# Head outputs turned by VectorE straight from a rotating output bank, in an attention and mixture-of-experts layer on one Trainium2 core

## The chip, the cores and the metric

One core of a Trainium2 chip runs the whole program. The metric is device time in microseconds (us) for one execution; a lower time is better. A timed run carries no profile. The profile is one further execution of the same program, taken by the hardware profiler, and its span is read on that execution alone.

Names used throughout: PE is TensorE (PEld its weight loads), DVE is VectorE, ACT is ScalarE, POOL is GpSimd, SP is SyncE, which here only issues DMAs. PSUM has eight banks of 128 partitions by 512 fp32 numbers.

## What is computed

Two sequences of 2048 tokens with 256 features pass through layer norm, 16-head attention (head dimension 16) with a local mixing term, and then a routed mixture of four experts. Cut to what matters here:

```python
Q, K, V = heads(x @ Wq.T + bq), heads(x @ Wk.T + bk), heads(x @ Wv.T + bv)
A = softmax(Q @ K.T / sqrt(16))                    # 2 sequences x 16 heads, 2048 x 2048 each
out = (0.6 * A + 0.4 * L) @ V                      # L: a fixed band of 7 tokens around the diagonal
x = x + out @ Wo.T + bo
x = x + experts(layernorm(x))                      # router, top 2 of 4 experts
```

The 32 pairs of a sequence and a head are called heads below.

## The kernel before

`project` (L153) normalises the tokens, projects Q and K and writes them in two pieces (a high and a low part in a short fp32 form) to a DRAM buffer `qk_pieces` (L232). `attend` (L367) then runs the 32 heads, two per pass of a loop, and `route_and_experts` does the rest.

For one head, `attend` goes through 16 steps `kb`, one for each 128 keys. In a step PE makes four score tiles (L763: 128 keys by 512 queries, chunks c = 0 to 3), which ACT exponentiates from PSUM into `probs` (L681), and multiplies the step's `probs` with the values (L775), adding into one output bank over the 16 steps. Four groups of 512 queries use four groups of 32 output partitions: 16 features, and 16 rows of ones that give the softmax sum. Score tiles rotate through three PSUM banks, so a tile waits for the exponential of the tile three before it. Scores are made one step ahead of the values.

The softmax needs the largest score of each query first. PE makes those scores as well (L750, two pairs per step, in four further banks, two for each pair) and DVE takes the row maxima of each pair with one reduction (L626). They run 21 steps ahead (`LOOK`): at step `kb` of head n, PE and DVE work on group kb + 5 of head n + 1. So at step 10 all 16 groups of head n + 1 are done; DVE combines and negates them (`split_shift`, L634), and POOL splits the result into two pieces (`split_shift`, L586 and L588). This `shift` (128 queries by 32 columns) must become rows of the score operand `score_q`, so it is transposed at the end of step 12 (`SHIFT_AT`): by PE (L782) into a score bank, copied by ACT to `shift_row` (L686), and written by four DMAs into `score_q` (`load_shift`, L484, `SHIFT_DMAS`). PE waits for these DMAs (`shift_in`, L842) at the start of step 15, where the scores of the next head begin.

At a head's end ACT copies the output bank to `heads_sb` (`copy_o`, L696), and PE's first values of the next head wait for that copy (L772). After step 1 (`HEADS_AT`) PE transposes `heads_sb` in four blocks of 128 x 128 (L786) into a score bank, and ACT copies it to `heads_tok` (`copy_tok`, L692). After the maxima of step 2 DVE inverts the softmax sums (`invert`, L642), and POOL multiplies them in (`normalise`, L597).

Every engine runs its own program in order, and the order is written out by hand; semaphores tie the programs together. SP issues, in order and per head: 12 loads of maximum operands, a store and two loads of weight chunks, the four shift DMAs, and 12 loads of score operands.

Of the kernel before, what the change touches and what calls it, by code (L numbers as in the profile page):

```python
# [152 lines left out]
def project(nc, ctx, dram, keep, block):  # L153
# [46 lines left out]
    def _(sp):  # L200
# [21 lines left out]
        for seq in range(BATCH):  # L222

            with sp.Fori(seq * BPS // 2, (seq + 1) * BPS // 2) as i:
                for u in range(2):
                    n = 2 * i + u
                    for qk in range(2):
                        for m in range(KD):
                            sp.wait_ge(piece_lo, QK * n + 2 * qk + m + 1)
                            head = seq * HEADS + m * (HEADS // KD)  # L230
                            dst = dram["qk_pieces"][qk, head:head + HEADS // KD, :, :, ds((n % BPS) * BLOCK, BLOCK)]
                            sp.dma_start(dst.rearrange("h d c t -> (h d) c t"),  # L232
                                         pieces[u][:, qk, m, :, :].bitcast(F32)).then_inc(stored[u], 16)
# [98 lines left out]
    def _(pe):  # L332
# [14 lines left out]
        def body(i, first, last):  # L347
            for u in range(2):
                n = 2 * i + u
                pe.wait_ge(xnT_ready, n + 1)  # L350
                for qk in range(2):
                    if qk == 1 and not (last and u):
                        transposes(n + 1, 1 - u)
                    for m in range(KD):
# [3 lines left out]
                        for k in range(KD):  # L358
                            done = nc.tensor.matmul(ps_qk[j], w["qk"[qk]][:, k, m * P:(m + 1) * P],
                                                    xnT[:, ds(n, 1), k, :].squeeze(1),  # L360
# [6 lines left out]
def attend(nc, ctx, dram, keep, block):  # L367
# [25 lines left out]
    heads_sb = sb("heads_sb", [P, BLOCK])  # L393
    heads_tok = sb("heads_tok", [P, BLOCK])
    part_max, neg_max, shift, shift_row = (keep[n] for n in ("part_max", "neg_max", "shift", "shift_row"))
    inv_sum = sb("inv_sum", [P, ST])
    w_raw = sb("w_raw", [P, CHUNK])
    w_pair = sb("w_pair", [P, 2, CHUNK], F32R)
    psum = keep["psum"]
    ps_s = [psum[:, c, :] for c in range(3)]  # L400
    ps_o = psum[:, 3, :]
    ps_m = [psum[:, 4:6, :], psum[:, 6:8, :]]

    ps_tr = psum[:, 7, :]
    ps_shift = ps_s[2][0:PIECES * ST, 0:P]
# [3 lines left out]
    UNITS = CH * ST + 2  # L409
    HEADS_AT = 1  # L410

    def unit(n, kb, c, ends=False):

        after = (kb > HEADS_AT + 1) + (kb > SHIFT_AT + 1 and not ends)
        return n * UNITS, CH * kb + c + after

    def heads_unit(n):
        return n * UNITS, CH * (HEADS_AT + 2)

    def shift_unit(n):  # L420
        return n * UNITS, CH * (SHIFT_AT + 2) + 1

    def count_of(at):
        return at[0] + at[1] + 1

    def bank_of(at):
        return ps_s[at[1] % RING]
    SHIFT_DMAS = PIECES * ROW_TILES
# [17 lines left out]
    first_tr, first_copied = sem("first_shift_tr"), sem("first_shift_copied")  # L446
    s_ready, exp_done = sem("s_ready"), sem("exp_done")
    pv_done = sem("pv_done")
    o_copied = sem("o_copied")
    inv_ready = sem("inv_ready")  # L450
    last_tr, last_copied = sem("last_tr"), sem("last_copied")
# [9 lines left out]
    SHIFT_HALF = 2 * (ST + 1)  # L461
# [9 lines left out]
    BANKS_BEFORE_SHIFT = v_tiles_before(SHIFT_HALF) // 2  # L471
    ps_v = [ps_s[r % VB] for r in range(BANKS - 1)] + [ps_o]
# [6 lines left out]
    def _(sp):  # L479
        def load_shift(u):  # L480
            for h in range(ROW_TILES):
                for c in range(PIECES):
                    row, first = h * ROW_TILE + STACK + c, c * ST + h * ST // ROW_TILES
                    sp.dma_start(score_q[u][row:row + 1, :].bitcast(F32).rearrange("o (t q) -> o t q", q=P),  # L484
                                 shift_row[first:first + ST // ROW_TILES, :].bitcast(F32)).then_inc(shift_in[u], 16)
# [11 lines left out]
        sp.wait_ge(first_copied, 1)  # L497
# [17 lines left out]
        def body(i, last):  # L515
            for u in range(2):
# [8 lines left out]
                if not (last and u):  # L525
                    sp.wait_ge(exp_done, count_of(shift_unit(n)))
                    load_shift(1 - u)
                if not last:
                    sp.wait_ge(s_ready, count_of(unit(n, ST - 1, CH - 1)))
# [5 lines left out]
    def _(pool):  # L535
# [11 lines left out]
        nc.gpsimd.memset(heads_sb[:], 1.0).then_inc(o_copied, 1)  # L547
        pool.wait_ge(o_copied, 1)
# [31 lines left out]
        def split_shift(m):  # L580
            pool.wait_ge(shift_step, m + 1)
            if m == 1:
                pool.wait_ge(first_tr, 1)
            elif m > 1:
                pool.wait_ge(s_ready, count_of(shift_unit(m - 2)))
            nc.gpsimd.tensor_copy(shift[:, 0, :], neg_max[:]).then_inc(shift_hi, 1)  # L586
            pool.wait_ge(shift_hi, m + 1)
            nc.gpsimd.tensor_tensor(shift[:, 1, :], neg_max[:], shift[:, 0, :].bitcast(F32), ALU.subtract  # L588
                                    ).then_inc(shift_ready, 1)

        def normalise(n):
            tok = heads_tok[:].rearrange("p (c b e) -> p c b e", c=BT, b=BPS)
            inv = inv_sum[:].rearrange("p (c b) -> p c b", c=BT)
            pool.wait_ge(inv_ready, n + 1)
            out = o_sb[:, (n - 1) // HEADS, :, (n - 1) % HEADS, :] if n > 0 else keep["spare"]
            out = out.rearrange("p (b c) d -> p c b d", c=BT)
            nc.gpsimd.tensor_tensor(out, tok[:, :, :, 0:HD], inv.unsqueeze(3).broadcast_to([P, BT, BPS, HD]),  # L597
# [23 lines left out]
    def _(dve):  # L621
# [15 lines left out]

        def invert(n):
            tok = heads_tok[:].rearrange("p (c b e) -> p c b e", c=BT, b=BPS)
            inv = inv_sum[:].rearrange("p (c b) -> p c b", c=BT)  # L640
            dve.wait_ge(exp_done, count_of(heads_unit(n)))
            nc.vector.reciprocal(inv, tok[:, :, :, HD]).then_inc(inv_ready, 1)  # L642

        for t in range(ST):
# [3 lines left out]
        nc.vector.tensor_copy(shift[:, 0, :], neg_max[:]).then_inc(shift_hi, 1)  # L648
        dve.wait_ge(shift_hi, 1)
        nc.vector.tensor_tensor(shift[:, 1, :], neg_max[:], shift[:, 0, :].bitcast(F32), ALU.subtract  # L650
                                ).then_inc(shift_ready, 1)
        for t in range(LOOK - ST):
            maxima(ST + t, t)

        def body(i, last):
            for u in range(2):
                n = 2 * i + u
                for kb in range(ST):
# [3 lines left out]
                    if kb == HEADS_AT + 1:  # L662
                        invert(n)
# [1089 lines left out]
```

## Time and profile before

| | before |
|---|---|
| timed runs, median of 3 | 1990.95 us (1990.76 to 1991.04) |
| span of the profiled execution | 2006.8 us |
| PE busy | 1951.3 us, 97% of the span |
| DVE busy | 1626.5 us, 81% |
| ACT busy | 1374.2 us, 68% |
| POOL busy | 346.9 us, 17% |

The profiled execution took 2006.8 us from its first to its last instruction, 15.9 us (0.8%) more than the median of the timed runs. The busy shares are means over stages with different limits: the attention heads run from about 130 us to 1431 us, the projections before and the experts after. Matmuls are pipelined and their ends are modelled, so the starts of instructions tell more than their durations.

### The profile page before, as it was taken

Reading aid. Unit: us, or ns where it says so; the run is one execution under the profiler, and the core shown is the slowest. Engines: PE = TensorE matmul, PEld = TensorE weight load, DVE = VectorE, ACT = ScalarE, POOL = GpSimd, SP = SyncE. Lnnn points to the kernel's source line nnn. Section 1 sums busy time; section 2 is a strip of 40 time slices with the busy share of each in tenths; the row PEclk is TensorE's granted clock in tenths of the full one; section 3 lists DMA queues with packets and bytes.
Section 4 is the critical chain, followed back from the end, with each engine's and each line's share of the span. In section 5 each row is a group of like instructions: output and inputs, shape, how many; then the busy total and the mean of one; then the engine's idle time right before and its main releaser. Section 6 shows DMA issues by size and latency. Waiting matters only on the chain. (4 is left out here: it accounts for less than half of the span.)

```text
span 2006.8 us, 47862 instructions
## 1 busy us (share of the span) xinstructions
PE 1951.3 (97%) x16384; PEld 1036.7 (52%) x16384; DVE 1626.5 (81%) x2075; ACT 1374.2 (68%) x2471; POOL 346.9 (17%) x379
## 2 busy tenths in 40 slices
PE   7999999999999999999999999999998799999997
PEld 3543333333333333333333333333687689999997
DVE  6799999999999999999999999994255565555564
ACT  3358888888888888888888888889544422233332
POOL 1361010001000100001000100010024532232233
PEclk9999999999999999999999999999999899999999
DMA  7954355335643454336534554341123677788884
GB/s 266 245 111 92 78 102 115 74 74 97 108 90 74 90 99 106 74 80 102 113 74 74 100 105 90 74 93 54 42 74 131 242 235 227 245 269 297 263 272 113
DMA packets 105849, 264.09 MB, mean 132 GB/s; under 512 B 20896, under 2 KB 52768, under 8 KB 99104
## 3 DMA queue, kind: packets, MB, share of 16 engines
q1 hardware_dynamic: 92624, 245.29, 48.6%
q0 software_dynamic: 13152, 17.83, 4.6%
q8 instruction: 44, 0.72, 0.1%
q14 instruction: 29, 0.24, 0.0%
HBM read 206.95 MB, written 73.94 MB: 140 GB/s over the span
## 5 line engine op out<-in xcount | busy, mean ns | idle before, releaser
L626 DVE TENSOR_REDUCE part_max<-psum 128x1 f32<-128x1024 f32 x1024 | 1240.8, 1222 | 50.6 <-PE psum L750 37.7
L681 ACT ACTIVATE probs<-psum 128x512 f32<-128x512 f32 x2048 | 1111.1, 596 | 145.4 <-PE psum L763 78.2
L763 PE MATMUL psum<-score_q,score_k 50*128 50x512 f32 x2048 | 745.9, 446 | 0.1
L750 PE MATMUL psum<-max_k,max_q 48*128 48x512 f32 x2048 | 737.9, 449 | 0.5 <-DVE part_max L626 0.4
L775 PE MATMUL psum<-probs,v_ones 128*32 128x256 f32 x8192 | 654.1, 391 | 9.4 <-ACT heads_sb L696 9.0
L763 PEld LDWEIGHTS psum<-score_q,score_k 50*128 50x128 f32 x2048 | 306.9, 184 | 404.7 <-ACT probs L681 390.7
L775 PEld LDWEIGHTS psum<-probs,v_ones 128*32 128x32 f32 x8192 | 162.1, 107 | 380.8 <-issue 198.1
L750 PEld LDWEIGHTS psum<-max_k,max_q 48*128 48x128 f32 x2048 | 294.2, 185 | 12.8 <-issue 7.0
L1184 ACT ACTIVATE x_sb<-psum,x_sb 128x512 f32<-128x512 f32 (+1 forms) x160 | 101.6, 636 | 257.8 <-PE psum L1564 243.1
L1583 PE MATMUL psum<-w,h_hi 128*128 128x256 f32 x1120 | 202.1, 279 | 2.7 <-DVE h_lo L1385 2.5
L1583 PEld LDWEIGHTS psum<-w,h_hi 128*128 128x128 f32 x1120 | 178.7, 189 | 13.8 <-DVE h_lo L1385 3.2
L1383 DVE CAST h_hi<-x_sb 128x512 fp32r<-128x512 f32 (+1 forms) x160 | 66.2, 414 | 129.2 <-ACT x_sb L1184 127.3
L1583 PE MATMUL psum<-w,h_lo 128*128 128x256 f32 x560 | 156.0, 278 | 0.0
L586 POOL CAST shift<-neg_max 128x16 fp32r<-128x16 f32 x31 | 6.1, 198 | 580.7 <-DVE neg_max L634 580.7
L1583 PEld LDWEIGHTS psum<-w,h_lo 128*128 128x128 f32 x560 | 105.3, 188 | 0.0
L1385 DVE TENSOR_TENSOR h_lo<-x_sb,h_hi 128x512 fp32r<-128x512 f32 (+1 forms) x160 | 100.2, 626 | 5.5
L1564 PE MATMUL psum<-w_end,w 128*128 128x512 f32 (+1 forms) x320 | 95.2, 379 | 2.2 <-ACT x_sb L1184 2.2
L1564 PE MATMUL psum<-route_xT_hi,w 128*128 128x512 f32 (+1 forms) x320 | 90.3, 363 | 0.0
L1121 POOL DMA_INDIRECT out<-x_sb,token x36 | 56.7, 1575 | 136.8 <-DVE x_sb L1403 95.5
L1121 POOL DMA_INDIRECT out<-attnT,token x34 | 53.5, 1574 | 140.1 <-DVE attnT L1403 93.4
L551 POOL COPY v_ones<-v_sb 128x256 f32<-128x256 f32 x32 | 12.8, 398 | 336.0 <-PE psum L775 335.8
L1097 POOL DMA_INDIRECT xs<-xrow,slot_at x64 | 63.4, 990 | 32.1 <-issue 19.7
(185 smaller groups left out, 1352.3 us busy)
## 6 DMA issues: line engine op xcount, KB each, us to landing
w<-w_split SPq DMA_DIRECT2D x40, 2048.0 KB, 7.9
max_q<-qk_pieces SPq DMA_DIRECT2D x192, 128.0 KB, 7.2
score_k<-qk_pieces SPq DMA_DIRECT2D x192, 128.0 KB, 4.7
xs<-in_pads SPq DMA_DIRECT2D x33, 528.0 KB, 8.3
qk_pieces<-pieces SPq DMA_DIRECT2D x32, 512.0 KB, 4.6
w_split<-w_pair SPq DMA_DIRECT2D x32, 512.0 KB, 8.8
max_k<-qk_pieces SPq DMA_DIRECT2D x192, 64.0 KB, 8.2
score_q<-qk_pieces SPq DMA_DIRECT2D x192, 64.0 KB, 2.2
```

Source lines behind the costliest of these rows:

```text
L626: nc.vector.tensor_reduce(part_max[:, t, p:p + 1], ps_m[p].rearrange("q b f -> q (b f)"), axis=AXIS.X, op=ALU.max).then_inc(m_read, 1)
L681: nc.scalar.activation(probs[kb % 2][:, chunk * BLOCK:(chunk + 1) * BLOCK], bank_of(at), ACT.Exp, scale=float(HD) ** -0.5).then_inc(exp_do ...
L750: last = nc.tensor.matmul(ps_m[p][:, h, :], max_q[u][rows, t * P:(t + 1) * P], max_k[u][rows, p * BLOCK:(p + 1) * BLOCK], start=True, stop ...
L763: nc.tensor.matmul(bank_of(at), score_k[u][rows, kb * P:(kb + 1) * P], score_q[u][rows, part * BLOCK:(part + 1) * BLOCK], start=True, stop ...
L775: last = nc.tensor.matmul(ps_o[QUAD * j:QUAD * (j + 1), at:at + BLOCK // PARTS], v_ones[u][:, kb, :], probs[kb % 2][:, j * BLOCK + at:j * ...
L1097: nc.gpsimd.indirect_dma_start(dram["xs"], bass.IndirectOffsetOnAxis(ap=at, axis=0), xrow[i % XROWS][:, t, :], None).then_inc(scattered[i ...
L1121: nc.gpsimd.indirect_dma_start(dram["out"], bass.IndirectOffsetOnAxis(ap=token[i % TOKEN_SETS][:, t:t + 1], axis=0), y[u][:, t, :], None, ...
L1184: nc.scalar.activation(h[m % H][:, 0:n], ps_h[m % PS_H][:, 0:n], ACT.Gelu, bias=biases[i % 2][:, m:m + 1]).then_inc(gelu_done, 1)
L1383: nc.vector.tensor_copy(h_hi[m % HALVES][:, 0:n], h[m % H][:, 0:n]).then_inc(h_hi_ready, 1)
L1385: nc.vector.tensor_tensor(h_lo[m % HALVES][:, 0:n], h[m % H][:, 0:n], h_hi[m % HALVES][:, 0:n].bitcast(F32), ALU.subtract).then_inc(h_lo_r ...
L1564: last = nc.tensor.matmul(ps_h[m % PS_H][:, 0:n], w[u][:, 2 * k + m // 4, c, at:at + P], xx[:, k, 0:n], start=j == 0, stop=j == len(terms) ...
L1583: last = nc.tensor.matmul(ps_y[u][:, t // 2, (t % 2) * DIM:(t % 2 + 1) * DIM], hs[m % HALVES][:, toks], w[u][:, chunk, c, at:at + DIM], st ...
```

## The change

VectorE's transpose turns each block of 32 x 32 by itself. The change makes that usable and drops the transposes by TensorE and the copies by ScalarE around them:

- The queries of a head are stored in another order: the Q projection reads its 512 tokens in an order that puts the 32-token quarters of the four 128-token tiles side by side, and each Q store goes to four separate stretches of 128 tokens instead of one of 512. Queries that are 32 apart in a block of the output bank are then the ones that VectorE's blocks need.
- The output bank alternates between PSUM banks 2 and 3 with the head (`OUT_OF`), and the three score banks rotate around it (`FIRST_RING`, `RING_OF`). `copy_o`, the four transposes of `heads_sb`, `copy_tok` and `heads_sb` go. VectorE turns the output bank into `heads_tok` (`turn_heads`) after the maxima of step 15, and inverts the sums after the maxima of the next head's step 0.
- PE's third score tile of step 1 (issued in step 0) takes the bank that held the last head's output and waits for `heads_turned`. The second tile of step 1 waits for the exponential of the tile two before it, where the others wait for the one three before.
- The shift is turned by VectorE too (`turn_shift`, after the maxima of step 12), with no copy by ScalarE. The result lies on 128 partitions, so `load_shift` has eight DMAs of 16 pieces of 128 bytes where it had four of eight pieces of 512 bytes.

```diff
-                            dst = dram["qk_pieces"][qk, head:head + HEADS // KD, :, :, ds((n % BPS) * BLOCK, BLOCK)]
...
+                            if qk == 0:
+                                dst = rows.rearrange("p c (j n) -> p c j n", j=BPS)[:, :, :, ds((n % BPS) * P, P)]
+                                src = src.rearrange("p c (j n) -> p c j n", j=BPS)
...
+                            if qk == 0:
+                                rows = rows.rearrange("p (b j r) -> p j b r", b=BT, j=BPS)
...
+    FIRST_RING, RING_OF, OUT_OF = ((0, 1, 2), (1, 0, 3)), ((1, 0, 3), (0, 1, 2)), (2, 3)
...
+    SHIFT_DMAS = ROW_TILES * P // QUAD
...
         def load_shift(u):
+            n = PIECES * ST // ROW_TILES
             for h in range(ROW_TILES):
-                for c in range(PIECES):
-                    row, first = h * ROW_TILE + STACK + c, c * ST + h * ST // ROW_TILES
-                    sp.dma_start(score_q[u][row:row + 1, :].bitcast(F32).rearrange("o (t q) -> o t q", q=P),
-                                 shift_row[first:first + ST // ROW_TILES, :].bitcast(F32)).then_inc(shift_in[u], 16)
+                row = h * ROW_TILE + STACK
+                dst = score_q[u][row:row + PIECES, :].bitcast(F32).rearrange("c (t q) -> c t q", q=P)
+                for q in range(P // QUAD):
+                    sp.dma_start(dst[:, :, q * QUAD:(q + 1) * QUAD],
+                                 shift_row[q * QUAD + h * n:q * QUAD + (h + 1) * n, :]).then_inc(shift_in[u], 16)
...
-                    sp.wait_ge(exp_done, count_of(shift_unit(n)))
+                    sp.wait_ge(shift_turned, n + 2)
                     load_shift(1 - u)
...
+        def turn_shift(m):
+            dve.wait_ge(shift_ready, m + 1)
+            nc.vector.transpose(shift_row[:], shift[:].rearrange("p h c t -> p (h c t)").bitcast(F32)
+                                ).then_inc(shift_turned, 1)
+
+        def turn_heads(n, u):
+            dve.wait_ge(pv_done, ST * (n + 1) + PV_OPEN)
+            dve.wait_ge(tok_used, n + 1)
+            nc.vector.transpose(heads_tok[:].rearrange("p t e -> p (t e)"), out_bank(u)).then_inc(heads_turned, 1)
...
-                    if kb == HEADS_AT + 1:
+                    if kb == INVERT_AT:
                         invert(n)
                     if ahead == ST - 1 and not (last and u):
                         split_shift(n + 1)
+                    if kb == SHIFT_AT and not (last and u):
+                        dve.wait_ge(shift_in[u], 16 * SHIFT_DMAS * (i + 1))
+                        turn_shift(n + 1)
+                turn_heads(n, u)
...
-        def copy_shift(at):
-            act.wait_ge(s_ready, count_of(at))
-            nc.scalar.activation(shift_row[:], bank_of(at)[0:PIECES * ST, 0:P], ACT.Copy).then_inc(exp_done, 1)
...
-        def copy_o(n):
-            act.wait_ge(pv_done, ST * (n + 1) + PV_OPEN)
-            nc.scalar.activation(heads_sb[:], ps_o, ACT.Copy).then_inc(o_copied, 1)
...
+        def scores(n, kb, u, c):
+            if kb == 1 and c == RING - 1:
+
+                pe.wait_ge(heads_turned, n + 1)
+            else:
+
+                held = 2 if kb == 1 and c == 1 else RING
+                if not isinstance(n, int) or s_done(n, kb, c) > held:
+                    pe.wait_ge(exp_done, s_done(n, kb, c) - held)
...
-                    if kb == HEADS_AT:
-                        wait_bank(heads_unit(n))
-                        pe.wait_ge(o_copied, n + 1)
-                        transpose_heads(bank_of(heads_unit(n))).then_inc(s_ready, 1)
-                    if kb == SHIFT_AT and not ends:
-                        wait_bank(shift_unit(n))
-                        wait_apart(pe, count, shift_ready, n + 2, ones_set, POOL_SET)
-                        transpose_shift(bank_of(shift_unit(n))[0:PIECES * ST, 0:P]).then_inc(s_ready, 1)
```

## Rows read from the trace of the kernel before

**Rows 1.** Windows: us, then busy us of each engine, clock, DMA share, GB/s.
```profile
600.00:800.00 200.00, 198.60 (x1917) 74.74 (x1909) 192.08 (x168) 176.05 (x330) 16.45 (x30) 1.00 0.48 93
60.00:80.00 20.00, 20.00 (x62) 10.11 (x60) 9.54 (x14) 8.17 (x12) 0.00 (x0) 1.00 1.05 396
```
**Rows 2.** The page's groups: busy us, mean ns of one, idle before, releaser.
```profile
L626 DVE TENSOR_REDUCE part_max<-psum 128x1 f32<-128x1024 f32 x1024 | 1240.8, 1222 | 50.6 <-PE psum L750 37.7
L750 PE MATMUL psum<-max_k,max_q 48*128 48x512 f32 x2048 | 737.9, 449 | 0.5 <-DVE part_max L626 0.4
```
**Rows 3.** PE timeline at a head's end: start, us, engine, line, idle before.
```profile
699.32 0.50 PE L763 MATMUL psum<-score_q,score_k 50*128 50x512 f32 x1
...
699.66 0.40 PE L763 MATMUL psum<-score_q,score_k 50*128 50x512 f32 x1
700.33 0.64 PE L775 MATMUL psum<-probs,v_ones 128*32 128x256 f32 x8 [0.27 <-ACT heads_sb L696]
700.90 0.50 PE L763 MATMUL psum<-score_q,score_k 50*128 50x512 f32 x1
```
**Rows 4.** PE timeline around the two transposes by TensorE.
```profile
691.68 0.28 PE L782 MATMUL psum<-ident_sb,shift 128*32 128x128 f32 x1
691.89 0.50 PE L763 MATMUL psum<-score_q,score_k 50*128 50x512 f32 x1
...
704.62 0.66 PE L786 MATMUL psum<-ident_sb,heads_sb 128*128 128x128 f32 x4
705.20 0.50 PE L763 MATMUL psum<-score_q,score_k 50*128 50x512 f32 x1
```
**Rows 5.** Timeline of DVE: maxima, the inversion, the combined maximum.
```profile
690.12 2.35 DVE L626 TENSOR_REDUCE part_max<-psum 128x1 f32<-128x1024 f32 x2
698.85 2.46 DVE L626 TENSOR_REDUCE part_max<-psum 128x1 f32<-128x1024 f32 x2
708.35 0.24 DVE L642 RECIPROCAL inv_sum<-heads_tok 128x16 f32<-128x16 f32 x1
728.64 4.62 DVE L626 TENSOR_REDUCE part_max<-psum 128x1 f32<-128x1024 f32 x4
```
**Rows 6.** Lines by form: a DVE instruction that reads 512 columns of PSUM.
```profile
L1363 DVE TENSOR_TENSOR route_xT_lo<-psum,route_xT_hi 128x512 fp32r<-128x512 f32 x3 | 2.1, 691 | 1.2 <-ACT route_xT_hi L1158 1.2
```
**Rows 7.** Timeline of the shift's way: ACT's copy, SP's four issues, PE's step 15.
```profile
692.00 0.27 ACT L686 ACTIVATE shift_row<-psum 32x128 fp32r<-32x128 f32 x1
692.29 2.73 SPq L484 DMA_DIRECT2D score_q<-shift_row  x4
696.84 0.50 PE L763 MATMUL psum<-score_q,score_k 50*128 50x512 f32 x1
```
**Rows 8.** Lines of SP's DMA issues: ns min/median/max, first and last start.
```profile
L484 SPq DMA_DIRECT2D score_q<-shift_row x128: 620/634/842, 119.6 to 1385.9; - x128
L122 SPq DMA_DIRECT2D max_k<-qk_pieces x192: 315/316/423, 54.2 to 1318.0; - x192
DMA to landing us min/median/max: 2.0/5.9/9.3
```
**Rows 9.** Windows around the last packets of the four shift DMAs.
```profile
695.60:695.90 0.30, 0.30 (x6) 0.29 (x4) 0.30 (x1) 0.30 (x1) 0.00 (x0) 1.00 0.06 14
```
**Rows 10.** ACT timeline: the last exponentials of a head, and the copy behind them.
```profile
698.61 1.09 ACT L681 ACTIVATE probs<-psum 128x512 f32<-128x512 f32 x2 [0.15 <-PE psum L763]
699.58 0.60 ACT L696 ACTIVATE heads_sb<-psum 128x512 f32<-128x512 f32 x1
```
**Rows 11.** PE timeline and windows behind the attention: two long idle stretches, the clock.
```profile
1575.32 1.22 PE L1513 MATMUL psum<-route_xT_hi,w_r_hi 128*128 128x512 f32 x2 [2.64 <-ACT rh L1165]
1609.78 0.50 PE L1583 MATMUL psum<-w,h_hi 128*128 128x256 f32 x2 [2.54 <-DVE h_lo L1385]
1574.88:1578.29 3.41, 2.97 (x7) 2.39 (x8) 2.24 (x13) 0.97 (x2) 2.68 (x3) 0.50 0.81 281
1609.00:1612.40 3.40, 2.62 (x17) 2.45 (x18) 3.30 (x8) 0.69 (x1) 2.48 (x4) 1.00 0.92 305
```

More of the change, by code:

```diff
@@ L408, in attend, with s_done, score_bank, out_bank @@
     RING = 3
[L409 to L428, printed above, removed]
+    UNITS = CH * ST
+    INVERT_AT = 0
+    FIRST_RING, RING_OF, OUT_OF = ((0, 1, 2), (1, 0, 3)), ((1, 0, 3), (0, 1, 2)), (2, 3)
+    def s_done(n, kb, c):
+        return n * UNITS + CH * kb + c + 1
+    def score_bank(u, kb, c):
+        at = CH * kb + c
+        return psum[:, FIRST_RING[u][at % RING] if at < CH else RING_OF[u][(at - CH) % RING], :]
+    def out_bank(u):
+        return psum[:, OUT_OF[u], :]
+    SHIFT_DMAS = ROW_TILES * P // QUAD
     PARTS = 2
@@ L469, in v_tiles_before @@
         return spread if half < FIRST_SCORES else min(TILES, TILES - 2 + half - FIRST_SCORES)
-    BANKS_BEFORE_SHIFT = v_tiles_before(SHIFT_HALF) // 2
-    ps_v = [ps_s[r % VB] for r in range(BANKS - 1)] + [ps_o]
+    ps_v = [psum[:, r % VB, :] for r in range(BANKS - 1)] + [psum[:, OUT_OF[1], :]]
     def v_tiles(b, vb):
@@ L701, in copy_v @@
                                  ).then_inc(v_copied, 1)
-        with act.Fori(0, BANKS_BEFORE_SHIFT // VB) as b:
+        with act.Fori(0, BANKS // VB - 1) as b:
             for vb in range(VB):
-                copy_v(b, vb, ps_s[vb])
-        for r in range(BANKS_BEFORE_SHIFT // VB * VB, BANKS - 1):
-            if r == BANKS_BEFORE_SHIFT:
-                act.wait_ge(first_tr, 1)
-                nc.scalar.activation(shift_row[:], ps_shift, ACT.Copy).then_inc(first_copied, 1)
-            copy_v(r // VB, r % VB, ps_v[r])
+                copy_v(b, vb, ps_v[vb])
+        copy_v(BANKS // VB - 1, 0, ps_v[0])
         for c in range(CH):
-            exp(0, 0, c, False)
+            exp(0, 0, 0, c)
             if c == 1:
-                copy_v((BANKS - 1) // VB, (BANKS - 1) % VB, ps_o)
+                copy_v(BANKS // VB - 1, 1, ps_v[BANKS - 1])
         def body(i, last):
@@ L779, in values @@
                 last.then_inc(pv_done, 1)
-        def transpose_shift(out):
-            return nc.tensor.transpose(out, shift[:].rearrange("p c t -> p (c t)").bitcast(F32), ident[:])
-        def transpose_heads(out):
-            for c in range(BT):
-                last = nc.tensor.transpose(out[:, c * P:(c + 1) * P], heads_sb[:, c * P:(c + 1) * P], ident[:])
-            return last
         def project_v(r, t):
@@ L829, in body @@
                 n = 2 * i + u
-                ends = last and u == 1
                 pe.wait_ge(v_in, n + 1)
@@ L843, in body @@
                     if more_scores:
-                        scores(*nxt, 0, ends)
+                        scores(*nxt, 0)
                     if more_maxima:
@@ L847, in body @@
                     if more_scores:
-                        scores(*nxt, 1, ends)
-                    values(n, kb, u, 0, ends)
+                        scores(*nxt, 1)
+                    values(n, kb, u, 0)
                     if more_scores:
-                        scores(*nxt, 2, ends)
+                        scores(*nxt, 2)
                     if more_maxima:
@@ L854, in body @@
                     if more_scores:
-                        scores(*nxt, 3, ends)
-                    values(n, kb, u, 1, ends)
-                    if kb == HEADS_AT:
-                        wait_bank(heads_unit(n))
-                        pe.wait_ge(o_copied, n + 1)
-                        transpose_heads(bank_of(heads_unit(n))).then_inc(s_ready, 1)
-                    if kb == SHIFT_AT and not ends:
-                        wait_bank(shift_unit(n))
-                        wait_apart(pe, count, shift_ready, n + 2, ones_set, POOL_SET)
-                        transpose_shift(bank_of(shift_unit(n))[0:PIECES * ST, 0:P]).then_inc(s_ready, 1)
+                        scores(*nxt, 3)
+                    values(n, kb, u, 1)
         twice(pe, pairs, body)
```

114 lines of the change are left out of this document (39 added, 75 removed).

## Prediction

> **What bounds the kernel now.** I read the windows first, to see which engine has room in the stage that the change touches. In the attention, PE is busy 198.6 of 200 us and DVE 192.1 [rows 1], which looks like two engines at their limit. The page's groups and DVE's timeline take that apart. PE waited for DVE's maxima 0.4 us in all, and DVE for PE 37.7 us [rows 2]. Two of DVE's reductions in the steady stretch take 2.46 us together; with 1.22 us for one [rows 2] they start 1.24 us apart. Four behind the combined maximum, which made DVE late, take 4.62 us and so start (4.62 - 1.22) / 3 = 1.13 us apart [rows 5]: DVE can catch up by 0.1 us at each. So PE sets the pace, at about 1.24 us for half a step (two score tiles, one maximum pair, half the values), and 32 halves are 39.7 us. The shift DMAs of 32 heads start from 119.6 to 1385.9 us [rows 8], 40.8 us per head. The difference of 1.1 us is what PE does or waits for besides. That is the stake of the change: per head it can win this, and not the busy time of ACT, which lies beside PE.
>
> **What goes, part by part.** At a head's end the half step from 699.32 to 700.90 us takes 1.58 us, with an idle of 0.27 us until ACT's copy is done [rows 3]: 0.34 us over a plain half. The four transposes of the heads take from 704.62 to 705.20: 0.58 us. The transpose of the shift takes 0.21 us, from 691.68 to 691.89 [rows 4]. Together 1.13 us per head on the path that sets the end. ACT's copies give nothing beyond that except in the last head, where no maxima run and ACT sets the pace: two copies, about 0.5 us of issue distance each, so 1 us once. At the very end one more group of four transposes goes, 0.5 us.
>
> **What the head's end costs after it.** The second score tile of step 1 now needs the exponential of the tile two before it, the last one of step 0. ACT's last pair of exponentials ends at 698.61 + 1.09 = 699.70 [rows 10]; today that tile's matmul starts at 699.66. From the end of ACT's copy, 700.18 [rows 10], to the values that waited for it, 700.33 [rows 3], pass 0.15 us; so the tile can start at 699.85, and 0.2 us are lost. A gain is excluded, since the tile waits for more than now; above, 0.34 us bounds it, today's wait, which had ACT's copy in front as well.
>
> The turn of the output bank is one DVE instruction over 128 x 512 of PSUM, which the trace does not show. The nearest row takes 0.69 us for 512 columns out of PSUM [rows 6]; twice the price per column would be 1.23. DVE reaches it when the last reduction of step 15 ends, the first of the two from 698.85, at 700.08 [rows 5], by which time the head's last values are long through; so the wait for them costs nothing. Turned at 700.77, it frees the bank that PE's third tile wants at 700.90 - 0.34 + 0.20 = 700.76: just hidden. Queued behind it on DVE are the maxima of the next step, 0.7 us late; their banks are wanted one half step later, and DVE's 0.1 us per half step pays it back. At twice the price PE would wait 0.55 us per head. The inversion (0.24 us) only moves from step 2 to step 0, and `normalise` on POOL with it, which has a whole head of time.
>
> **What the shift costs.** This is the part that decides. Today ACT's copy ends at 692.27, SP issues four DMAs from 692.29 for 2.73 us, and PE starts step 15 at 696.84 without a wait [rows 7]. One issue takes 0.634 us (0.620 to 0.842) [rows 8], so they lie (2.73 - 0.63) / 3 = 0.70 us apart, and the last begins at 694.39. Its packets still move after 695.6 [rows 9], 1.2 to 1.5 us later; other loads on this queue landed after 2.0 us at the least [rows 8]. I take 1.8 us, keep 1.4 to 2.2, and so have the four landed at 696.2, 0.6 us before they are wanted.
>
> After the change DVE reaches the turn when the maxima of step 12 are read, at 690.12 + 2.35 = 692.47 [rows 5]. A short DVE instruction, the inversion, takes 0.24 us from 708.35 [rows 5]; part of it can lie beside the reduction before, so the turn adds 0 to 0.24, I take 0.16. SP starts 0.02 us later, as behind ACT today: 692.65. It now issues eight DMAs, not four. At 0.70 us each the last begins at 692.65 + 7 x 0.70 = 697.55 and lands at 699.35. PE, 0.21 us earlier than today, stands at step 15 at 696.63. PE waits 2.7 us, and with it everything: the score tiles of the next head are the first thing in step 15, and the maxima, the values, DVE and ACT are all queued behind them. Nothing covers this.
>
> The price of one issue is the unknown: the new ones have other shapes (16 pieces of 128 bytes, two destination rows). The cheapest issues of this queue take 0.315 us [rows 8]; with the same 0.07 us between them the last lands at 697.1 and PE waits 0.5 us. At 0.842 it is 700.8, and 4.2 us. I take 0.634, the row of the same two tensors. The Trainium skill speaks against the change here: "DMA: Bandwidth & Descriptors", section "Rules for kernel authors", asks to coalesce many small transfers, since below 64 KB mostly overhead is paid. The change splits the same 16 KB into twice as many.
>
> The wait occurs at 30 heads. For the last head DVE has no maxima after step 10, so its turn comes two steps earlier. SP's later loads slide by some 3 us and have tens of microseconds.
>
> **Small things.** The first shift has eight DMAs too, with DVE turning about 1 us earlier than ACT copied: I add 1 us. The Q stores move 512-byte pieces where they moved 2 KB; the DMA share is 1.05 from 60 to 80 us, while PE stays busy throughout [rows 1]: 0 to 3 us, I take 0.5.
>
> **The sum.** 30 x 2.7 = 81.0; 31 x (0.20 - 1.13) = -28.8; the 32nd group of head transposes -0.6, ACT in the last head -1.0, the end -0.5, the first shift 1.0, the Q stores 0.5. That is +51.6 us on the profiled execution, whose span of 2006.8 us stands 0.8% over the median; I add it to the median unscaled: 2043.
>
> **The clock.** PE has no idle stretch like 2.7 us in the attention today. Behind it there are some. After 2.64 us of idle the granted clock was 0.50, the level of 1.2 GHz, from 1574.88 to 1578.29; after 2.54 us it stayed at 1.00 [rows 11]. One such stretch of 3.4 us at half the clock costs PE, which is the bound here, 1.7 us of work. With one row each way I can only bound it: 0 to 30 times 1.7, 0 to 51 us. I take a third of the heads, as PE is otherwise never idle here, so +17: 2060.
>
> **The rivals.**
> - Faster: the eight issues are cheap. Place: SP between steps 12 and 15. Without any wait the sum is 51.6 - 81.0 = -29.4, so it decides at a wait of 29.4 / 30 = 1.0 us, which is a distance of 0.45 us per issue. At the cheapest row's 0.38 the wait is 0.5 us: 30 x 0.5 - 29.4 = -14, so 1977. For it: 315 ns rows on the same queue. Against: 128 issues of this very transfer never took less than 620. Chance 0.11.
> - Faster still: the issues don't count at all and the wait stays hidden, 2043 - 81 = 1962. The Trainium skill has this rule, "DMA: Bandwidth & Descriptors", section "Issuing engines are not separate DMA queues": the sequencer's time to start a DMA is usually small beside the DMA. The rows of this transfer speak against it, 0.63 us of issue for 4 KB. Chance 0.03.
> - The head's end becomes the bound: the turn costs twice as much and PE waits 0.55 us more per head, 31 x 0.55 = 17, 2077 with the wait for the shift. It lies inside the forecast's range.
> - The clock falls at every wait: 2043 + 51 = 2094. With the dearest issues (30 x 1.5 more) beyond 2106. Chance of over 2106: 0.06.
> - The change does its work but the terms cancel, a wait of about 1.0 us: 1991, chance 0.03.
>
> **How the numbers follow.** The forecast, eight issues at the row's price and the clock falling at none to all heads, has the remaining 0.77. The range: from 2043 down by 12 for the early landing (30 x 0.4) and by 25 for issues some 0.12 us cheaper, 2006; up by 51 for the clock and by 12 for the late landing, 2106. A measurement of this kernel can tell about 0.2% from no change, 4 us. Faster 0.14, same 0.03, slower 0.83.
>
> **What would show it.** Right: PE idle 2 to 3 us once per head at L763's first tile of step 15, released by the shift DMAs; heads 42 to 44 us apart; 1.24 us per half step elsewhere; no idle over 0.4 us at the head's end; DVE no dearer than 0.7 us for the turn; stretches at half clock behind some of the waits. Wrong: SP's eight issues within 3 us, or heads 40 us apart; then the price of an issue was the failed step. A wait of PE for `heads_turned` would show the turn's price wrong.

## The result and the profile after

| | before | after |
|---|---|---|
| median of the runs, us | 1990.86 | 2241.32 (four runs, 2200.30 to 2267.90) |
| span of the profiled execution, us | 2006.8 | 2266.1 (that run: 2267.90) |

The change makes the kernel slower: the ratio is 1.113, 95% interval 1.105 to 1.121. The four runs of after differ by 3%, and their mean granted clock with them (0.871 in the profiled run of 2267.90 us, 0.906 in that of 2200.30); the ratio and its interval are of the two shortest, 2200.30 and 2232.51 us. The forecast was 2060 us, 2006 to 2106. Its sign was right and its size wrong: about 180 us more were lost by the median. The profile of after, like those of the experiments and unlike that of before, belongs to one of the timed runs.

The page of the kernel after: the span, the busy lines, PE and its granted clock in 40 slices, then two groups (busy us, mean ns of one, idle before, releaser).

```profile
span 2266.1 us, 47389 instructions
...
PE 2159.4 (95%) x16220; PEld 1080.6 (48%) x16220; DVE 1648.4 (73%) x2139; ACT 1340.0 (59%) x2374; POOL 346.4 (15%) x379
...
PE   8999999999999999999999999999999989999997
...
PEclk9998767687988877779879996878899999999999
...
L740 PE MATMUL psum<-score_q,score_k 50*128 50x512 f32 x2048 | 874.2, 511 | 72.6 <-DMA score_q<-shift_row 72.5
...
L725 PE MATMUL psum<-max_k,max_q 48*128 48x512 f32 x2048 | 852.5, 512 | 0.8 <-DVE part_max L620 0.8
```

Three things are to be seen. The wait that was forecast is there: 72.5 us in front of the score tiles, released by the shift DMAs, 72.3 of them in 30 waits of 2.34 to 2.55 us. PE is busy nearly all the same, 95% of a span that is 13% longer. And one maxima matmul, which took 449 ns before [rows 2], now takes 512 in the mean. The clock line, in tenths of full speed, says why: it falls below 9 in most slices of the attention.

One head shows how this hangs together. First the way of the shift on DVE and SP's queue, then PE (start, us, engine, line, idle before in brackets):

```profile
1225.29 0.20 DVE L634 STREAM_TRANSPOSE shift_row<-shift 128x32 f32<-128x32 f32 x1
...
1225.52 5.27 SPq L484 DMA_DIRECT2D score_q<-shift_row  x8
```

```profile
1227.08 0.50 PE L740 MATMUL psum<-score_q,score_k 50*128 50x512 f32 x1
...
1228.32 0.50 PE L740 MATMUL psum<-score_q,score_k 50*128 50x512 f32 x1
...
1231.97 0.49 PE L740 MATMUL psum<-score_q,score_k 50*128 50x512 f32 x1 [2.34 <-DMA score_q<-shift_row]
...
1233.49 0.79 PE L740 MATMUL psum<-score_q,score_k 50*128 50x512 f32 x1
...
1235.65 0.79 PE L740 MATMUL psum<-score_q,score_k 50*128 50x512 f32 x1
...
1239.97 0.50 PE L740 MATMUL psum<-score_q,score_k 50*128 50x512 f32 x1
```

Up to the wait, half steps begin 1.24 us apart; 1.5 us behind it they begin 2.16 us apart, and each matmul takes half as long again or more. The windows of the same stretch (us, busy us of each engine, granted clock, DMA share, GB/s) show the clock behind it:

```profile
1229.63:1231.97 2.34, 0.00 (x0) 0.01 (x1) 0.69 (x1) 0.31 (x1) 0.00 (x0) 1.00 0.02 3
...
1233.10:1239.90 6.80, 6.80 (x44) 2.11 (x36) 4.76 (x5) 3.75 (x7) 2.22 (x3) 0.50 0.91 147
1239.97:1260.00 20.03, 20.03 (x198) 7.49 (x196) 19.52 (x18) 17.20 (x32) 0.62 (x1) 1.00 0.63 125
```

Behind 2.34 us without work, PE gets the level of 1.2 GHz for 6.80 us, in which it is busy throughout, and then 2.4 GHz again. In the whole attention 29 of the 30 waits are followed by such a stretch, of 3.4 to 37.5 us, 566.6 us in all. A half step takes 2.16 us at the lower level and 1.23 at the upper, so a stretch loses 1 - 1.23/2.16 = 43% of its length: 244 us. With 72 us of waits that is 316, and some 30 us should be won elsewhere, which leaves 286. Between the run of this profile and the median of before lie 277 us. (The two spans differ by 259, but the span of before stood 15.9 us over its timed runs.)

### The profile page after: what moved, and what is told of

It is laid out like the page before. It is cut to its first block and busy times, and to the rows that moved or that the text cites. A ratio compares the mean times of both kernels' runs of the same rounds, so it can differ in the third digit from the quotient of the medians.

```text
span 2266.1 us, 47389 instructions
## 1 busy us (share of the span) xinstructions
PE 2159.4 (95%) x16220; PEld 1080.6 (48%) x16220; DVE 1648.4 (73%) x2139; ACT 1340.0 (59%) x2374; POOL 346.4 (15%) x379
## 5 line engine op out<-in xcount | busy, mean ns | idle before, releaser
L740 PE MATMUL psum<-score_q,score_k 50*128 50x512 f32 x2048 | 874.2, 511 | 72.6 <-DMA score_q<-shift_row 72.5
L725 PE MATMUL psum<-max_k,max_q 48*128 48x512 f32 x2048 | 852.5, 512 | 0.8 <-DVE part_max L620 0.8
L750 PE MATMUL psum<-probs,v_ones 128*32 128x256 f32 x8192 | 766.2, 451 | 0.4 <-ACT probs L686 0.4
L740 PEld LDWEIGHTS psum<-score_q,score_k 50*128 50x128 f32 x2048 | 359.5, 215 | 597.9 <-ACT probs L686 475.3
L750 PEld LDWEIGHTS psum<-probs,v_ones 128*32 128x32 f32 x8192 | 172.0, 115 | 442.8 <-issue 313.1
L725 PEld LDWEIGHTS psum<-max_k,max_q 48*128 48x128 f32 x2048 | 342.7, 215 | 13.2 <-issue 7.0
```

Of the source, the lines that this page charges most:

```text
L725: last = nc.tensor.matmul(ps_m[p][:, h, :], max_q[u][rows, t * P:(t + 1) * P], max_k[u][rows, p * BLOCK:(p + 1) * BLOCK], start=True, stop ...
L740: nc.tensor.matmul(score_bank(u, kb, c), score_k[u][rows, kb * P:(kb + 1) * P], score_q[u][rows, part * BLOCK:(part + 1) * BLOCK], start=T ...
L750: last = nc.tensor.matmul(out_bank(u)[QUAD * j:QUAD * (j + 1), at:at + BLOCK // PARTS], v_ones[u][:, kb, :], probs[kb % 2][:, j * BLOCK + ...
```

## The experiments

The theory: the eight issues make the wait, and the wait, by leaving PE idle, brings the lower clock; the rest of the change is as good as forecast. The rivals: the turned outputs and the changing banks slow PE themselves; the clock falls for the DMAs or for something else that stands at the same place. Times are medians.

**The whole change, the wait moved out of the way.**

```diff
-SHIFT_AT = 12
+SHIFT_AT = 11
```

> The whole change, but VectorE turns the shift behind the maxima of step 11, not of step 12, about 2.45 us earlier. In the profile of the kernel after, TensorE stands 2.34 to 2.55 us at the first score product of step 15, 30 times (72.5 us), and 29 of these waits are followed by a stretch at the half level (566.6 us in all, where a half step takes 2.16 us and not 1.23). Theory 1, the wait brings the half level: one step of lead shortens each wait to 0.0 to 0.2 us, the half level is gone from the attention stage, and of the 2268 us of that profile some 70 us of waits and some 243 us of slow half steps go: 1950 to 1970 us, faster than both kernels. Theory 2, the turned outputs and the changing banks bring the half level (or slow TensorE) by themselves: the waits go, the half level stays, and the time stays above 2150 us. Theory 3, the waits go and the half level with them, but the end of a head now waits for VectorE's 0.71 us turn: 30 times up to 1 us, 1970 to 2000 us.

Measured: 1969.24 us (ratio to the kernel before 0.988, 0.9865 to 0.9898). The page:

```profile
span 1967.4 us, 47389 instructions
...
PEclk9999999999999999999999999999999999999999
...
L740 PE MATMUL psum<-score_q,score_k 50*128 50x512 f32 x2048 | 755.7, 447 | 4.6 <-DMA score_q<-shift_row 3.2
```

One step of lead takes the wait from 72.5 to 3.2 us, and with it every half-level stretch of the attention. Theory 1 holds, at the upper end of its bounds; theory 2 falls, for banks and turns are all still there. The two variants of the change, at 1.113 and 0.988 of the kernel before, differ in the place of one 0.20 us instruction and in nothing else.

**The kernel before, with eight issues and nothing else of the change.**

```diff
-    SHIFT_DMAS = PIECES * ROW_TILES
+    SHIFT_DMAS = 2 * PIECES * ROW_TILES
...
-                    sp.dma_start(score_q[u][row:row + 1, :].bitcast(F32).rearrange("o (t q) -> o t q", q=P),
-                                 shift_row[first:first + ST // ROW_TILES, :].bitcast(F32)).then_inc(shift_in[u], 16)
+                    for g in range(2):
+                        at, half = first + g * BPS, slice(g * BLOCK, (g + 1) * BLOCK)
+                        sp.dma_start(score_q[u][row:row + 1, half].bitcast(F32).rearrange("o (t q) -> o t q", q=P),
+                                     shift_row[at:at + BPS, :].bitcast(F32)).then_inc(shift_in[u], 16)
```

> The kernel before with one thing changed: each of the four shift DMAs is split in two (four of its eight rows each), so that eight issues of some 0.6 to 0.7 us follow one another on SyncE and not four; TensorE still turns the shift, ScalarE still copies it, nothing else of the change is in it. Theory 1, the issues alone make the wait and the wait brings the half level: the last DMA is issued some 2.5 to 2.7 us later, TensorE stands 1.8 to 2.6 us at the first score product of step 15 (the chain of before had up to 0.6 us of room), the half level follows most of these waits: 2180 to 2320 us. Theory 2, the issues make the wait, but the half level belongs to the rest of the change: 1991 + 30 x 1.8 to 2.6 = 2045 to 2070 us. Theory 3, the issues are hidden here, and the wait of the change comes from its turn or its queue: 1985 to 1997 us.

Measured: 2223.72 us (2187.23 to 2232.27), theory 1. A head of it, SP's queue and PE, and the page's clock and group:

```profile
217.04 5.08 SPq L486 DMA_DIRECT2D score_q<-shift_row  x8
...
223.38 0.50 PE L765 MATMUL psum<-score_q,score_k 50*128 50x512 f32 x1 [1.71 <-DMA score_q<-shift_row]
...
224.79 0.79 PE L765 MATMUL psum<-score_q,score_k 50*128 50x512 f32 x1
```

```profile
PEclk9979887889598869897889998979859999999999
...
L765 PE MATMUL psum<-score_q,score_k 50*128 50x512 f32 x2048 | 841.9, 501 | 49.6 <-DMA score_q<-shift_row 47.6
```

The waits are 1.52 to 1.99 us here (31, 48 us; for the last, 1.99 us, the profile names no releaser), shorter than I expected, and 24 of them are followed by the lower level; these stretches hold 440.3 us. So four more issues per head are enough to turn the kernel before into one as slow as the kernel after, without any turn by DVE.

**The wait filled with work.** In the wait at step 15 PE multiplies the identity into the bank that the next score tile overwrites; the shift's DMAs stay where they are.

```diff
+BUSY = 11
...
+                        pe.wait_ge(exp_done, s_done(n + 1, 0, 0) - RING)
+                        spare = score_bank(1 - u, 0, 0)
+                        for r in range(BUSY):
+                            nc.tensor.matmul(spare[:, (r % BT) * P:(r % BT + 1) * P], ident[:], ident[:],
+                                             start=True, stop=True)
                         pe.wait_ge(shift_in[1 - u], 16 * SHIFT_DMAS * (i + 1 + u))
```

> The change as it is, but TensorE doesn't stand still in the wait at step 15: ahead of the wait for the shift DMAs it multiplies the identity with itself into the bank that the next score product overwrites, 11 products of 128x128 fp32, by the rows some 0.2 us each, 2.3 us in all. The shift's DMAs and their time stay, only TensorE's idleness goes. Theory 1, idleness brings the half level: the waits still cost some 72 us (products and rest together), the half level is gone from the attention stage: 2268 - 243 = about 2025 us in the terms of the kernel after's profile, 2010 to 2050. Theory 2, something else brings the half level (the DMAs into the score rows, the changing banks): 2180 to 2280 us, half level behind most heads as before.

Measured: 2199.00 us (ratio 1.104), as theory 2 would have it. The trace shows that it is a miss of the experiment, and a useful one. PE around the filled wait at 208.38, and two half steps later:

```profile
208.38 2.72 PE L809 MATMUL psum<-ident_sb 128*128 128x128 f32 x22
211.03 0.50 PE L741 MATMUL psum<-score_q,score_k 50*128 50x512 f32 x1
...
216.50 0.49 PE L741 MATMUL psum<-score_q,score_k 50*128 50x512 f32 x1 [2.92 <-issue]
...
218.19 0.79 PE L741 MATMUL psum<-score_q,score_k 50*128 50x512 f32 x1
```

The products fill the wait, with no idle time behind them, and 31 filled waits are followed by the lower level only where another idle time comes in between: two half steps later, where the next pass of the two-head loop begins, PE now stands 2.60 to 3.38 us though it waits for nothing that the profile shows ("issue"); the run with the earlier turn has no idle time at this place. All 14 of these are followed by a stretch at 0.50, 314 us in all. They are no wait for the shift's DMAs, and the clock falls behind them all the same. What goes with them stands among the DMA queues of the page, first of this run, then of the next one (packets, MB, share of 16 engines):

```profile
q8 instruction: 170, 2.79, 0.6%
```

```profile
q8 instruction: 43, 0.70, 0.1%
```

The queue that moves instructions carries 170 packets of 16 KB here and 43 or 44 in every other kernel of this document. Between 225 and 1320 us it moves 101 in this run and none in the others. At each of the 14 stops such a packet is on its way as the stop begins: at the one shown it starts at 213.33, lasts 1.40 us, and PE stands from 213.58 to 216.50. So the longer program has its instructions brought anew in every pass of the loop, and the stop at the turn goes with that; that PE waits for this packet is my reading, since the profile names no releaser.

**The same with three wide products in place of eleven.** The products take an operand from a weight, and PE waits for it once, ahead of the heads (`route_in`).

```diff
+BUSY = 3
...
+        pe.wait_ge(route_in, 16 * 5)
...
+                        pe.wait_ge(exp_done, s_done(n + 1, 0, 0) - RING)
+                        for r in range(BUSY):
+                            nc.tensor.matmul(score_bank(1 - u, 0, 0), ident[:], w_r1[:, 0, :], start=True, stop=True)
                         pe.wait_ge(shift_in[1 - u], 16 * SHIFT_DMAS * (i + 1 + u))
```

> As the run with identity products, with fewer and wider ones: in the wait at step 15 TensorE makes 3 products of 128x512 fp32 in place of 11 of 128x128. There, the 22 records of each wait took 2.65 us, no idle time was left at the first score product and no half level followed; but once per turn of the two-head loop TensorE then stood 2.6 to 3.1 us with nothing that it waited for (its program had grown), and the half level followed these (14 stretches, 314 us in all). Theory 1, idleness of any origin brings the half level and a busy wait keeps it off: with 3 instructions and not 11 the stop at the loop's turn goes back to 0.2 us, no half level is left, and the time is 1969 + 30 x 2.5 = about 2045 us (2035 to 2060). Theory 2, the half level follows the shift's DMAs or the loop's turn however busy TensorE is: 2150 to 2230 us.

Measured: 2046.30 us (2046.00 to 2047.30, ratio 1.027), theory 1. The page:

```profile
PEclk9999999999999999999999999999999999999999
...
L741 PE MATMUL psum<-score_q,score_k 50*128 50x512 f32 x2048 | 752.9, 447 | 0.4 <-DMA score_q<-shift_row 0.3
...
L809 PE MATMUL psum<-w_r,ident_sb 128*128 128x512 f32 x186 | 88.1, 610 | 0.0
```

The same eight DMAs, the score tile still held up (2.77 us from the first product to that tile, 85.9 us in all), and no lower level in the attention. It is now the three products that hold the tile up, and no longer the DMAs, for which PE waits 0.3 us in all. So it is in part luck that the time comes so near to what the sum of the prediction gave without the clock, 2043, with 81 us of waits. Useless work in the wait brings the ratio from 1.113 to 1.027.

**How long an idle time?** Two runs make the idle piece shorter, in different ways. In one the turn of the shift stands between the two maxima of step 12:

```diff
-        def maxima(g, t):
+        def maxima(g, t, between=None):
...
             for p in range(2):
+                if p == 1 and between is not None:
+                    between()
                 dve.wait_ge(m_ready, 2 * g + p + 1)
...
-                        maxima(ST * (n + 1) + ahead, ahead % ST)
+                        maxima(ST * (n + 1) + ahead, ahead % ST, turn if here else None)
```

> The whole change, but the shift's turn stands between the two maxima of step 12, not behind them: one half step (1.23 us) earlier, so that TensorE's waits at step 15 should last 1.1 to 1.4 us and not 2.34 to 2.55 us, 30 times, 33 to 42 us. This asks from which idle time on the half level follows. Theory 1a, an idle time of 1.2 us doesn't bring it: 1962 + 38 = about 2000 us, 1985 to 2010. Theory 1b, it does, behind most waits: 2150 to 2250 us. Theory 1c, it does behind some: between 2010 and 2150 us, by the share of waits that a half level follows (some 8 us each).

Measured: 2046.54 us (2032.55 to 2058.22, ratio 1.028), theory 1c, near its lower end. In the other, the filled wait has one wide product and not three:

```diff
-BUSY = 3
+BUSY = 1
```

> As the run with three wide products in the wait at step 15, with one: it keeps TensorE busy for some 0.9 us (the six records of three products took 2.8 us), and of each wait of 2.34 to 2.55 us some 1.4 to 1.7 us stay idle, in one piece behind the product. The waits and their DMAs cost the same, 30 x 2.4 to 2.6 us. Theory 1, the idle piece counts: TensorE idle 1.21 to 1.40 us was followed by the half level 4 times in 30 (the turn between step 12's maxima), 1.52 to 1.99 us 24 times in 31 (eight issues in the kernel before), so here between 4 and 24 of 30, some 8 us each: 2045 + 32 to 190 = 2075 to 2235 us. Theory 2, the length of the stop from one score product to the next counts, whatever lies in it: 29 of 30, 2200 to 2270 us. Theory 3, any product in the wait keeps the half level off: 2035 to 2050 us.

Measured: 2065.29 us (2058.63 to 2085.42, ratio 1.036), a little under the lower end of theory 1. The score tile still comes 2.43 us behind the product in the median, but 1.13 us of this are busy. Theory 2 falls: the length of the stop is not what counts. Theory 3 falls too. The groups of the two, in this order:

```profile
L746 PE MATMUL psum<-score_q,score_k 50*128 50x512 f32 x2048 | 773.8, 457 | 38.5 <-DMA score_q<-shift_row 38.4
```

```profile
L741 PE MATMUL psum<-score_q,score_k 50*128 50x512 f32 x2048 | 778.9, 461 | 38.3 <-DMA score_q<-shift_row 38.2
```

All runs together, for the waits of the attention in the profiled executions:

| idle of PE in one piece, us | kernel | followed by 0.50 | us at 0.50 |
|---|---|---|---|
| 0.07 to 0.28 | whole change, turn at step 11 | 0 of 30 | 0 |
| 0.67 to 0.69 | head turned twice (below) | 0 of 30 | 0 |
| 1.20 to 1.39 | filled with one product | 7 of 30 | 122.9 |
| 1.21 to 1.40 | turn amid step 12 | 4 of 30 | 88.7 |
| 1.52 to 1.99 | before with eight issues | 24 of 31 | 440.3 |
| 2.34 to 2.55 | after | 29 of 30 | 566.6 |
| 2.60 to 3.38 | filled with eleven, loop's turn | 14 of 14 | 314.0 |

The mean stretch is 18 to 22 us long in each of them; what grows with the idle time is how often one follows. Each row is one execution, and the 7 and the 4 of 30 are no clear difference: the profiled run of the kernel with one product had the lowest mean granted clock of its four (0.967, the others 0.975 to 0.981). Left out of the table is the first head's wait in the kernel before with eight issues, 1.21 us from 123.78 on, while V is still projected: 27.3 us at 0.50 follow it.

**Is the turn of the head hidden?** The version with the early shift turn, and the head's outputs turned twice:

```diff
-SHIFT_AT = 12
+SHIFT_AT = 11
...
+            nc.vector.transpose(heads_tok[:].rearrange("p t e -> p (t e)"), out_bank(u)).then_inc(again, 1)
+            dve.wait_ge(again, n + 1)
             nc.vector.transpose(heads_tok[:].rearrange("p t e -> p (t e)"), out_bank(u)).then_inc(heads_turned, 1)
```

> The version with the shift turned at step 11 (1969 us), with the head's outputs turned twice, one turn behind the other: VectorE works 0.71 us more at each head's end, 32 times. Theory 1, the turn lies beside other work: between maxima that queue up VectorE starts one every 1.13 us, and TensorE hands over one every 1.23 us, so it makes up 0.1 us in each, and the second turn is made up within the head; what TensorE loses is the later release of the output bank, which it wants one half step later: 0 to 0.3 us a head, 1969 to 1979 us. Theory 2, VectorE is the bound at the head's end: the whole second turn counts, 31 x 0.6 to 0.7 = +19 to +22 us, 1988 to 1991 us.

Measured: 1990.66 us, 21 us more than with one turn: theory 2, and I had expected the first. DVE and PE at a head's end:

```profile
659.13 0.71 DVE L641 STREAM_TRANSPOSE heads_tok<-psum 128x512 f32<-128x512 f32 x1
659.87 0.72 DVE L643 STREAM_TRANSPOSE heads_tok<-psum 128x512 f32<-128x512 f32 x1
```

```profile
660.64 0.49 PE L743 MATMUL psum<-score_q,score_k 50*128 50x512 f32 x1 [0.68 <-DVE heads_tok L643]
```

PE waits for the bank 30 times, 20.4 us in all, nearly the whole second turn. My expectation looked at DVE's room for its maxima, which is there; but PE wants the bank as the first turn ends, so the first is hidden with nothing to spare.

**The shift turned one half step earlier still**, between the maxima of step 11, with the hook of the run amid step 12:

```diff
-SHIFT_AT = 12
+SHIFT_AT = 11
```

> The version with the shift turned at step 11, with the turn between the two maxima of that step, one half step earlier. In the profile of that version TensorE still stands 3.2 us in all at the first score product of step 15 behind the shift's DMAs. Theory 1: these go, and the shift is ready by then (GpSimd was done 0.9 us behind the negative maxima): 1964 to 1968 us, no half level. Theory 2: the turn now waits for GpSimd's split and holds back the maxima behind it: 1969 to 1980 us.

Measured: 1959.84 us (ratio 0.984, 0.9824 to 0.985), the fastest of all and better than theory 1 said. Why the last 3.2 us of waits were worth 9 us is seen at PE's step 15. First the run with the turn behind step 11, then that with the turn amid it, there with the first half step of a head and step 15 of the same head:

```profile
646.14 0.49 PE L740 MATMUL psum<-score_q,score_k 50*128 50x512 f32 x1 [0.20 <-DMA score_q<-shift_row]
646.27 0.59 PE L725 MATMUL psum<-max_k,max_q 48*128 48x512 f32 x2
...
647.50 0.49 PE L740 MATMUL psum<-score_q,score_k 50*128 50x512 f32 x1
```

```profile
645.89 0.49 PE L746 MATMUL psum<-score_q,score_k 50*128 50x512 f32 x1
...
646.33 0.50 PE L746 MATMUL psum<-score_q,score_k 50*128 50x512 f32 x1
...
647.33 0.50 PE L746 MATMUL psum<-score_q,score_k 50*128 50x512 f32 x1
...
683.02 0.50 PE L746 MATMUL psum<-score_q,score_k 50*128 50x512 f32 x1
683.03 0.73 PE L731 MATMUL psum<-max_k,max_q 48*128 48x512 f32 x2
...
684.26 0.50 PE L746 MATMUL psum<-score_q,score_k 50*128 50x512 f32 x1
```

In the steady stretch the score tile and the maxima matmul start together. A wait of 0.20 us parts the two, and the half steps around it lost 0.38 and 0.28 us to a plain one at two successive heads. In the second fence step 15 begins at 683.02 without a wait, its score tile and its maxima 0.01 us apart, and its half step takes 1.24 us. What is left per head is the half step at 645.89, 1.44 us for 1.23, in which the second score tile comes 0.44 us behind the first and not 0.34.

**The runs as a sum.** From 1960 us (the run with the turn amid step 11), with each profile's stops in front of the score tiles and 43% of its stretches at 0.50:

| kernel | stops | stretches | sum | its profiled run |
|---|---|---|---|---|
| three products | 85.9 | 0 | 2046 | 2046.0 |
| turn amid step 12 | 38.2 | 88.7 x 0.43 = 38.1 | 2036 | 2037.8 |
| one product | 72.8 | 122.9 x 0.43 = 52.8 | 2086 | 2085.4 |
| eleven products | 82.2 + 41.3 | 314.0 x 0.43 = 135.0 | 2218 | 2214.3 |
| after | 72.3 | 566.6 x 0.43 = 243.6 | 2276 | 2267.9 |

No other term is needed to come within 0.4% of all five. In the last one 25 of the 29 stretches begin while PE still waits, and 15.5 us count twice; without them it is 2269. The sum holds for the runs of after that have no list of stretches, too. Twice what the mean granted clock lacks to 1.00, times the span, gives the time at 0.50: 585 us in the profiled run, as its list does (566.6 in the attention and 17.9 behind it). In the three others it gives 526, 495 and 413 us, and so, less those 17.9, sums of 2251, 2237 and 2202 us; measured were 2250.12, 2232.51 and 2200.30.

## Why the prediction was wrong, point by point

**What bounds the kernel: right.** PE set the pace, at 1.23 us per half step (taken: 1.24), and each stop of PE came out in the end time, as the sum above shows.

**The eight issues: right, a little too dear.** I took 0.634 us per issue, 0.70 apart, 1.8 us to the landing, 2.7 us of wait. In the trace of after the issues take 601 to 856 ns, median 611. In the head shown they lie (5.27 - 0.61) / 7 = 0.67 us apart, and the last begins at 1225.52 + 4.66 = 1230.18, 1.79 us before PE goes on. The waits are 2.34 to 2.55 us: 72 us in place of 81. The rivals with cheap or hidden issues fall. The rule on small transfers that I cited from the Trainium skill, "DMA: Bandwidth & Descriptors", section "Rules for kernel authors", asks to coalesce many small transfers. The runs agree: splitting the transfers of the kernel before in two, and nothing else, took it from 1991.60 us to 2187.23 at the least, though only 48 us of this are waits. The Trainium skill's rule in "DMA: Bandwidth & Descriptors", section "Issuing engines are not separate DMA queues", is that the sequencer's time to start a DMA is usually small beside the DMA. It doesn't fit this transfer: eight issues fill 5.27 us, and PE goes on 1.79 us after the last has begun.

**The head's end: right.** The turn takes 706 ns (taken: 0.69), and PE waits for it 0.4 us in all. The second score tile loses 0.21 us per head (taken: 0.20), read in the run with the turn amid step 11, in which the shift's wait doesn't hide it. All terms but the waits came to -29.4 us, that is 1961.5; that run gives 1959.8, 32.1 us under the kernel before as measured beside it. The rival in which the turn costs twice as much didn't come; the run with two turns shows that its mechanism, PE waiting for the bank, was real and one turn away.

**The clock: the step that failed.** I had two rows behind the attention, 2.64 us of idle with a half-level stretch of 3.41 us, and 2.54 us without [rows 11]. From these I took a fall behind a third of the waits, and 1.7 us for each: 17 us, at most 51. The trace of after has a fall behind 29 of 30, and a mean stretch of 566.6 / 29 = 19.5 us, which costs 8.4 us: 244 us. The share was off by a factor of three, the price by five. The price was the worse error: I took the length of the one stretch at hand for the length of all. The trace of before has two more such stretches in the same part of the program, each of 3.4 us as well, but none in the attention, where PE's work is another; why the stretches are longer there the runs don't show. The share of a third had no row behind it. The bound of 51 us was no bound, since only the number of falls was varied in it and not their length: the rival in which the clock falls at every wait had the share nearly right and came to 2094 us at that price. With the measured clock the sum of the prediction, 2043, becomes 2287, of which the dearer issues that I took explain 9; the profiled run gave 2268. In the run of 2200.30 us, by its mean granted clock, the term is 170 us and not 244, still ten times what I took.

## What to carry to other kernels

Where TensorE is the bound and is never idle, a wait that a change brings can cost more than its length: here waits of 2.4 us cost 10.5 us per head, while those of 0.7 us in the run with two turns cost hardly more than they lasted (20.4 us of waits, 21 us of time). Price such a wait with the clock behind it, and look first at whether the producer can be moved: one half step of lead (1.23 us) halved the wait, three of them took it away and made a change that was 11% slower into one that is 1.6% faster. Where it can't be moved, a few wide matmuls into a bank that is overwritten anyway can keep the clock up, if they leave no idle piece: with three nothing fell here, with one 7 of 30 waits were still followed by a fall, and with eleven the longer program brought stops of its own.

## What the runs showed of the hardware

The granted clock stayed at the 1.2 GHz level for up to 51 us though TensorE worked without a pause. The window of that stretch, in the kernel before with eight issues (one of 58.0 us in its last head has 0.25 us of pauses):

```profile
763.90:815.10 51.20, 51.20 (x288) 16.78 (x280) 28.81 (x25) 26.76 (x50) 2.84 (x4) 0.50 0.39 69
```

I can tie the return to nothing that the traces show; the stretches of after are 3.4 to 37.5 us long behind waits that hardly differ. What ends them was not tried.

In the kernel after, the fall came 1.5 to 4.2 us after the idle time had begun, in 25 cases while TensorE still waited and in 4 when it was at work again. What it costs stands behind the wait and not in it: whoever looks only at the waits finds 72 of the 316 us.

A program made longer by 11 unrolled matmuls per head stopped TensorE for 2.60 to 3.38 us at the turns of its loop, 14 times, with no semaphore that the profile names; with 3 matmuls this was gone. Packets of instructions moved in each pass of that loop, 101 between 225 and 1320 us, and none in the other kernels between these times.
